# Mamba-style scan block: the first sums of a chunk in two pieces, TensorE's side work in other slots, x loaded before the end of the scan phase

## The chip, the core and the metric

The kernel runs on one core of a Trainium2 chip. The metric is the time of one execution on the device, in microseconds (us), median of several runs. The core has five engines that run their own instruction streams and meet at semaphores: TensorE (PE; its weight loads are shown as PEld), VectorE (DVE), ScalarE (ACT), GpSimd (POOL) and SyncE (SP, which here only issues DMAs).

## What is computed

Eight images of 64x64 tokens with 96 channels go through two layers. The first is a selective state-space scan over four orders of the tokens (diagonal, anti-diagonal, and both backwards), the second a linear attention and a quantised feed-forward part. Only the scan matters for this change:

```python
def step(hst, inp):
    u_t, d_t, B_t, C_t = inp
    hst = hst * jnp.exp(d_t[..., None] * A) + (d_t * u_t)[..., None] * B_t[:, :, None, :]
    return (hst, jnp.einsum('bkdn,bkn->bkd', hst, C_t))
```

with 192 channels d, 16 states n, 4 orders k and 4096 tokens t. The decay is exp(d_t A), the drive is (d_t u_t) B_t, and the output is a sum over the 16 states of state times C_t.

## The kernel before, in words

**Tiling.** For each image the scan phase runs over 4 orders times 8 chunks of 512 tokens: 32 chunks an image, 256 in all. In a chunk the 192 x 16 pairs of channel and state are dealt with in 12 steps (`NSTEP`), each of two scans on 128 partitions (4 states x 32 channels). `GROUPS` says which 32 channels a step has: 4, 5, 0, 1, 2, 3 and again 4, 5, 0, 1, 2, 3. Groups 4 and 5 are the high channels, and their sums go to PSUM bank 5; groups 0 to 3 are the low ones, and go to bank 4. A group takes the 32 rows 32g (or 32(g-4)) of its bank, and so the 32 columns of TensorE's array with that number.

**One step.** ACT makes the decays (L671, two exponentials a step, three steps ahead of use); PE makes the drive (`fill`, L1002, 32 small matmuls, shown as 64 records since each float32 matmul has two), DVE runs the two scans (L1370), POOL multiplies the states by C (L484). PE then sums products over the states (`sum_states`, L1026): a batch is four steps, and each of its two halves a = 0, 1 is one call of four matmuls. After the sixth call of a chunk DVE adds the result to the image's output (`add_sums`, L1349 to L1357; it stands in DVE's stream between the two scans of step 5 of the next chunk, and waits for the semaphore `summed`).

**Order on PE.** PE's stream of a chunk has 12 slots. Slot s begins with the fill of step s + 2 (the fills of steps 0 and 1 of the next chunk in slots 10 and 11), since two steps fit into PSUM at once: that fill waits until DVE has scanned step s. Behind it stands the side work that the code hands to the slot: for the next chunk the projections (`project_lo` L959, `project_hi` L964, one for the high channels, v = 0, and one for the low, v = 1), the turned B (`turn_b`, L975), the turned product du (`turn_du`, L984); and the sums, by the table `SUM_SLOTS`, slot to (batch, a), where slots from `NSTEP` on are those of the next chunk. So before the change the slots hold, beside a fill each: 0 project_hi 0; 1 sum (2,0) of the chunk before; 2 turn_b; 3 project_hi 1 and sum (2,1) of the chunk before; 4 nothing; 5 sum (0,0); 6 turn_du 0; 7 sum (0,1); 8 turn_du 1; 9 project_lo 0; 10 sum (1,0); 11 sum (1,1) and project_lo 1.

**ACT beside the decays.** In slot 4 of its own stream it saves the turned B (L631), runs the two softplus (L615, each after its project_hi; between exponential and softplus it loads a table), and issues the DMAs that replicate the high channels' delta (L648). SP writes B to memory in a skewed layout (L375) when ACT has saved it, reads it back (L382), replicates the other delta (L399) and C (L390).

**Ends of the phase.** Before the first chunk of an image, `pre` runs the same side work with nothing to hide it. After the last chunk all engines meet (`rendezvous`), SP loads the image's x into `xtok` (L354), which lies on the same memory as `delta_rep`, and PE's first transposes of it (L1074) open the next phase.

Of the kernel before, what the change touches and what calls it, by code (L numbers as in the profile page):

```python
# [29 lines left out]
NCH = L // T  # L30
# [29 lines left out]
def build(nc, io, out, nb=B):  # L60
    ctx = ExitStack()
    with ctx:
# [99 lines left out]
        def rendezvous(eng, b, ph):  # L162

            eng.drain().then_inc(phase_done, 1)  # L164
            wait_apart(eng, phase_done, b * (NPH * ENGINES) + (ph + 2) * ENGINES)
# [100 lines left out]
            return bank(SMALL)[0:rows, at:at + cols]  # L266

        Y_BANK, HI_BANK, LO_BANK = 4, 6, 7
        SUM_SLOTS = {5: (0, 0), 7: (0, 1), 10: (1, 0), 11: (1, 1), NSTEP + 1: (2, 0), NSTEP + 3: (2, 1)}

        GROUPS = (4, 5, 0, 1, 2, 3) * NPR
        BT_ROWS = slice(DHI, P)
# [42 lines left out]
        def chunks(eng, b, body, pre):  # L315


            def at(kk, c, par, first=False):
                ch = Chunk(b, kk, c, first)
                ch.par = par  # L320
                return ch
            order = [at(kk, c, c % 2, kk == 0 and c == 0) for kk in range(K) for c in range(NCH)] + [None, None]
            pre(order[0], order[1])
            for ch, nx, then in zip(order, order[1:], order[2:]):
                body(ch, nx, then, 0 if ch.c == 0 else 1 if ch.c + 1 < NCH else 2)
# [3 lines left out]
        def _(sp):  # L329
# [27 lines left out]
            def load_x(sp, b):  # L357
                for c in range(NCH):
                    load_part(b, c)

            def image(b, f):
# [44 lines left out]
                    load_c(1)  # L406

                chunks(sp, b, lambda ch, nx, then, kind: prepare(nx) if nx else None, lambda ch, nx: prepare(ch))
                rendezvous(sp, b, 1)

                load_x(sp, b)
                wait_apart(sp, x_loaded, (b * 2 + 2) * (16 * NCH))
                if f is not None:
                    for c in range(NCH):
# [145 lines left out]
        def _(act):  # L560
# [44 lines left out]
            def image(b, f):  # L605
# [43 lines left out]

                def pre(ch, nx):  # L650
                    copy_bc(ch)
                    softplus(ch, 0)
                    softplus(ch, 1)
                    load_delta(ch, 4)
                    load_delta(ch, 5)
                    save_bt(ch)
                    save_du(ch, 0)
                    save_du(ch, 1)
                    for s in range(AHEAD):
                        decays(ch, s)  # L660
# [237 lines left out]
        def _(pe):  # L898
# [53 lines left out]
            def image(b, f):  # L952
# [8 lines left out]
                def project_hi(ch, v):  # L961

                    z = 1 - v
                    pe.matmul(bank(HI_BANK + v), xw_hi[:, ch.k, z * P:(z + 1) * P], u_hi[:, bass.ds(ch.t0, T)], start=False, stop=True).then_inc(pre_filled, 1)  # L964
# [50 lines left out]
                    project_lo(nx, 0)  # L1015
                    project_lo(nx, 1)

                def sum_states(ch, batch, a):

                    if batch == 0 and a == 0 and not ch.first:  # L1020
                        pe.wait_ge(y_saved, ch.n(2, 0))
                    pe.wait_ge(weighted, ch.n(NSTEP, 4 * batch + 4))
                    for s in range(4 * batch, 4 * batch + 4):
                        g = GROUPS[s]
                        bk, row = (Y_BANK, CW * g) if g < 4 else (Y_BANK + 1, CW * (g - 4))
                        mm = pe.matmul(bank(bk)[row:row + CW, :], gather[:, :], ch.weighed(s, a),  # L1026
                                       start=(s < NG and a == 0), stop=(s >= NG and a == 1))
                    if a == 1:
                        mm.then_inc(summed, 1)

                def body(ch, nx, then, kind):
                    if not ch.first:
                        kk, c = (ch.kk, ch.c - 1) if kind else (ch.kk - 1, NCH - 1)
                        before = Chunk(ch.b, kk, c)
                        before.par = 1 - ch.par
                    for s in range(NSTEP):
                        if s + 2 < NSTEP:
                            fill(ch, s + 2)
                        elif nx:
                            fill(nx, s + 2 - NSTEP)  # L1040
                        if nx:
                            if s == 0:
                                project_hi(nx, 0)
                            if s == 3:
                                project_hi(nx, 1)
                            if s == 2:
                                turn_b(nx)
                            if s == 6:
                                turn_du(nx, 0)
                            if s == 8:  # L1050
                                turn_du(nx, 1)
                            if s == 9 and then:
                                project_lo(then, 0)
                        if s in SUM_SLOTS:
                            sum_states(ch, *SUM_SLOTS[s])
                        if not ch.first and s + NSTEP in SUM_SLOTS:
                            sum_states(before, *SUM_SLOTS[s + NSTEP])
                        if s == NSTEP - 1 and then:
                            project_lo(then, 1)
                    if nx is None:  # L1060
                        sum_states(ch, 2, 0)
                        sum_states(ch, 2, 1)
# [558 lines left out]
```

## Time and profile before

| | before |
|---|---|
| median of 3 runs | 11323.54 us (11293.52 to 11373.81) |
| the profiled execution | 11306.72 us, its span 11304.9 us |
| TensorE clock granted, mean | 0.927 |
| PE busy | 9638.9 us, 85% |
| DVE busy | 8620.7 us, 76% |
| POOL busy | 7841.6 us, 69% |
| ACT busy | 6486.2 us, 57% |
| chain that ended last, by engine | PE 55%, issue 14%, DVE 11%, POOL 9% |

A row of the groups names line, engine, operation, what it writes and reads, its count, the time in which any of the group ran, the mean of one, then the idle time of the engine ahead of the group and what ended it. "issue" is idle time that no semaphore explains. The TensorE clock has two levels here, 2.4 GHz (1.0) and 1.2 GHz (0.5).

### The profile page before, as it was taken

How to read it: one execution, taken by the hardware profiler on the slowest of the kernel's cores; microseconds unless marked ns; L12 is line 12 of the kernel's file. 1: busy time of each engine (PE TensorE's matmuls, PEld its weight loads, DVE VectorE, ACT ScalarE, POOL GpSimd, SP SyncE). 2: the span in 40 equal slices, each digit the busy share in tenths (PEclk: the TensorE clock that was granted, in tenths of full speed). 3: DMA queues.
4: the chain of work that ended last, by engine and by line, in shares of the span. 5: the costliest groups of instructions: out<-in, count | busy, mean ns of one | idle time of the engine just before them, and what ended most of it. 6: DMA issues, size and time to landing. Idle time of an engine off the chain costs nothing.

```text
span 11304.9 us, 500467 instructions
## 1 busy us (share of the span) xinstructions
PE 9638.9 (85%) x224288; PEld 4968.1 (44%) x224288; DVE 8620.7 (76%) x8404; ACT 6486.2 (57%) x9893; POOL 7841.6 (69%) x4027
## 2 busy tenths in 40 slices
PE   7888888888888888888888888898888888888886
PEld 3444344443444434444344443444434444344443
DVE  4898668986589856899568895698956888478884
ACT  4666556665566645666456664566645666456664
POOL 3888538885488854888458884588845888458883
PEclk9999899998999989999889998899989999899997
DMA  3555225552255523555135551355513555145550
GB/s 90 148 147 147 64 77 143 149 141 62 81 142 153 141 55 84 147 149 152 40 96 144 147 148 38 98 146 148 147 35 110 146 143 145 28 116 149 143 144 22
DMA packets 853330, 1301.52 MB, mean 115 GB/s; under 512 B 517231, under 2 KB 518800, under 8 KB 785148
## 3 DMA queue, kind: packets, MB, share of 16 engines
q1 hardware_dynamic: 752892, 1135.15, 36.1%
q10 hardware_dynamic: 98304, 134.35, 4.5%
q8 instruction: 1776, 29.10, 1.2%
q14 instruction: 358, 2.93, 0.1%
HBM read 832.67 MB, written 33.55 MB: 77 GB/s over the span
## 4 chain that ended last, share of the span: by engine, by line
PE 55%; issue 14%; DVE 11%; POOL 9%; SPq 4%; ACT 3%; DMA 2%; ACTq 2%; POOLq 1%; DVEq 0%
PE ps L1002 22%; PE ps L1026 13%; DVE arena L1370 8%; PE ps L934 5%; PE ps L964 5%; POOL arena L484 5%; PE ps L959 4%; SPq L399 3%; PE ps L975 2%; ACTq L648 2%; ACT arena L671 1%; PE ps L984 1%; POOL arena L501 1%; POOL arena L509 1%; POOL arena L536 1%
## 5 line engine op out<-in xcount | busy, mean ns | idle before, releaser
L1370 DVE TENSOR_TENSOR_SCAN arena<-arena,ps 128x512 f32<-128x512 f32 x6144 | 7259.5, 1251 | 899.9 <-PE ps L1002 887.2
L484 POOL TENSOR_TENSOR arena<-arena 128x1024 f32<-128x1024 f32 x3072 | 6613.4, 2185 | 1414.1 <-DMA arena<-c_rows 979.4
L671 ACT ACTIVATE arena<-arena,negA 128x512 f32<-128x512 f32 x6144 | 3952.1, 714 | 1755.5 <-DMA arena<-arena 831.6
L1002 PE MATMUL ps<-arena 64*32 64x128 f32 x196608 | 3966.2, 284 | 1046.9 <-issue 479.5
L1002 PEld LDWEIGHTS ps<-arena 64*32 64x32 f32 x196608 | 2965.3, 107 | 3024.5 <-issue 2997.1
L1026 PE MATMUL ps<-arena,gather 128*32 128x512 f32 x12288 | 2207.4, 631 | 66.9 <-POOL arena L484 50.4
L934 PE MATMUL ps<-arena,wconv 96*64 96x512 f32 (+1 forms) x2304 | 835.9, 629 | 23.7 <-issue 23.7
L469 POOL TENSOR_TENSOR arena<-arena,u_hi 128x512 f32<-128x512 f32 x256 | 327.8, 1280 | 696.1 <-ACT arena L615 696.1
L1026 PEld LDWEIGHTS ps<-arena,gather 128*32 128x32 f32 x12288 | 374.4, 111 | 992.5 <-issue 808.8
L964 PE MATMUL ps<-u_hi,xw_hi 128*128 128x512 f32 x1024 | 671.0, 742 | 3.0 <-issue 3.0
L671 ACT ACT_TABLE_LOAD x256 | 328.4, 1283 | 557.9 <-issue 557.7
L959 PE MATMUL ps<-u_lo,xw_lo 128*128 128x512 f32 x1024 | 589.6, 660 | 55.2 <-SPq L164 47.2
L615 ACT ACTIVATE arena<-ps,dtb 128x512 f32<-128x512 f32 x512 | 341.8, 688 | 341.8 <-PE ps L964 338.2
L934 PEld LDWEIGHTS ps<-arena,wconv 96*64 96x64 f32 (+1 forms) x2304 | 301.9, 172 | 415.4 <-issue 407.9
L469 POOL TENSOR_TENSOR arena<-arena,u_lo 128x512 f32<-128x512 f32 x256 | 328.9, 1285 | 115.8 <-PE ps L984 101.9
L515 POOL TENSOR_TENSOR arena<-arena,power 128x4 f32<-128x4 f32 x64 | 64.8, 1013 | 425.7 <-DVE arena L1401 425.7
L639 ACT ACTIVATE arena<-ps 128x256 f32<-128x256 f32 (+1 forms) x512 | 247.0, 484 | 175.0 <-PE ps L984 174.4
L975 PE MATMUL ps<-ident,arena 16*64 16x16 f32 x4096 | 297.1, 209 | 48.3 <-issue 39.1
L615 ACT ACT_TABLE_LOAD x256 | 328.4, 1283 | 4.7
L984 PE MATMUL ps<-ident,arena 64*128 64x64 f32 (+1 forms) x2048 | 290.4, 264 | 41.5 <-POOL arena L469 34.0
L531 POOL TENSOR_TENSOR arena<-arena 128x1056 f32<-128x1056 f32 x16 | 64.4, 4024 | 372.0 <-DVE arena L1430 372.0
L975 PEld LDWEIGHTS ps<-ident,arena 16*64 16x64 f32 x4096 | 270.7, 138 | 115.2 <-issue 115.2
(155 smaller groups left out, 5648.4 us busy)
## 6 DMA issues: line engine op xcount, KB each, us to landing
arena<-b_runs SPq DMA_DIRECT2D x512, 1024.0 KB, 7.0
arena<-arena SPq DMA_DIRECT2D x4096, 64.0 KB
arena<-c_rows SPq DMA_DIRECT2D x2048, 128.0 KB, 3.8
arena<-arena ACTq DMA_DIRECT2D x2048, 64.0 KB
arena<-in_x SPq DMA_DIRECT2D x128, 192.0 KB, 2.7
out_tokens<-arena SPq DMA_DIRECT2D x64, 192.0 KB, 2.4
c_rows<-arena SPq DMA_DIRECT2D x256, 32.0 KB
b_runs<-arena SPq DMA_DIRECT2D x512, 16.0 KB
```

The costliest lines, as they stand in the source:

```text
L469: pool.tensor_tensor(du.rearrange("p (k h t) -> p h k t", h=2, k=NB), in_time(t_l[v]), in_time(u_lo[:, ch.dir, cols] if v else u_hi[:, col ...
L484: pool.tensor_tensor(ch.weighed(s)[:, :, flip], ch.span(s)[:, :, flip], c_row[:, :, flip], ALU.mult).then_inc(weighted, 1)
L615: act.activation(t_l[v], bank(HI_BANK + v), ACT.Softplus, bias=dtb[:, 1 - v, ch.k:ch.k + 1]).then_inc(delta_done, 1)
L671: act.activation(ch.span(s, a), delta_rep[:, g, :], ACT.Exp, scale=negA[:, ch.k, i:i + 1]).then_inc(decay_ready, 1)
L934: return pe.matmul(to.rearrange("p (r w) -> p r w", w=W), wconv[:, t, channels], xT_img[:, r0:r0 + ROWS, dx:dx + W], start=(t == 0), stop= ...
L959: pe.matmul(bank(HI_BANK + v), xw_lo[:, ch.k, z * P:(z + 1) * P], u_lo[:, ch.dir, bass.ds(ch.t0, T)], start=True, stop=False)
L964: pe.matmul(bank(HI_BANK + v), xw_hi[:, ch.k, z * P:(z + 1) * P], u_hi[:, bass.ds(ch.t0, T)], start=False, stop=True).then_inc(pre_filled, 1)
L975: mm = pe.matmul(to, bc_raw[r, steps(h, k)], ident[r, ch.d0:ch.d0 + NS].rearrange("p (q n) -> p q n", n=RUN), start=True, stop=True)
L984: mm = pe.transpose(bank(HI_BANK + v)[:, k * w:(k + 1) * w], du[r, k * P:(k + 1) * P], ident[r, r])
L1002: mm = pe.matmul(to, du_t[ch.par][rows, k, g * CW:(g + 1) * CW], spots[rows, j, :, :], start=True, stop=True)
L1026: mm = pe.matmul(bank(bk)[row:row + CW, :], gather[:, :], ch.weighed(s, a), start=(s < NG and a == 0), stop=(s >= NG and a == 1))
L1370: dve.tensor_tensor_scan(ch.span(s, a)[:, flip], ch.span(s, a)[:, flip], drive(s % 2)[:, :, a][:, flip], before, ALU.mult, ALU.add).then_i ...
```

## The change

Four edits:

1. `SUM_SLOTS`: the sums of the first batch (steps 0 to 3) go in pieces. Piece `half` 0 is steps 0 and 1 (groups 4, 5: high channels), piece 2 is steps 2 and 3 (groups 0, 1). (0,0) has its pieces in slots 5 and 6, (0,1) in slots 7 and 8. The semaphore `summed` is raised behind piece 2. The last sum (2,1) of the chunk before moves from slot 3 to slot 2.
2. PE's other side work: turn_b from slot 2 to 3, project_hi 1 from 3 to 4, turn_du 1 from 8 to 9.
3. `pre` on ACT: the turned B is saved right behind the copy of B and C, and the first half of du ahead of the delta DMAs.
4. SP: x is loaded when the last decays of the image have been made (they are the last to read `delta_rep`), ahead of the rendezvous.

```diff
-        SUM_SLOTS = {5: (0, 0), 7: (0, 1), 10: (1, 0), 11: (1, 1), NSTEP + 1: (2, 0), NSTEP + 3: (2, 1)}
+        SUM_SLOTS = {5: (0, 0, 0), 6: (0, 0, 2), 7: (0, 1, 0), 8: (0, 1, 2), 10: (1, 0), 11: (1, 1), NSTEP + 1: (2, 0), NSTEP + 2: (2, 1)}
...
+                wait_apart(sp, decay_ready, (b + 1) * (K * NCH * NCOL))
+                load_x(sp, b)
                 rendezvous(sp, b, 1)
 
-                load_x(sp, b)
...
                     copy_bc(ch)
+                    save_bt(ch)
                     softplus(ch, 0)
                     softplus(ch, 1)
+                    save_du(ch, 0)
                     load_delta(ch, 4)
                     load_delta(ch, 5)
-                    save_bt(ch)
-                    save_du(ch, 0)
                     save_du(ch, 1)
...
-                def sum_states(ch, batch, a):
-
-                    if batch == 0 and a == 0 and not ch.first:
+                def sum_states(ch, batch, a, half=None):
+
+                    if batch == 0 and a == 0 and half == 0 and not ch.first:
                         pe.wait_ge(y_saved, ch.n(2, 0))
                     pe.wait_ge(weighted, ch.n(NSTEP, 4 * batch + 4))
-                    for s in range(4 * batch, 4 * batch + 4):
+                    for s in range(4 * batch + (half or 0), 4 * batch + (4 if half is None else half + 2)):
...
-                    if a == 1:
+                    if a == 1 and half != 0:
                         mm.then_inc(summed, 1)
...
                             if s == 3:
+                                turn_b(nx)
+                            if s == 4:
                                 project_hi(nx, 1)
-                            if s == 2:
-                                turn_b(nx)
                             if s == 6:
                                 turn_du(nx, 0)
-                            if s == 8:
+                            if s == 9:
                                 turn_du(nx, 1)
```

On PE, in a chunk of the running loop, from slot 2 to the fill of slot 8, there stood before (L1002 fill, L975 turn_b, L964 project_hi, L1026 sum, L984 turn_du; x64 are two fills):

```order
L1002 MATMUL ps<-arena 32x128 x32
L975 MATMUL ps<-ident,arena 64x2x8 x8
L1002 MATMUL ps<-arena 32x128 x32
L964 MATMUL ps<-u_hi,xw_hi 128x512
L1026 MATMUL ps<-arena,gather 32x512 x4
L1002 MATMUL ps<-arena 32x128 x64
L1026 MATMUL ps<-arena,gather 32x512 x4
L1002 MATMUL ps<-arena 32x128 x32
L984 MATMUL ps<-ident,arena 128x64 x4
L1002 MATMUL ps<-arena 32x128 x32
L1026 MATMUL ps<-arena,gather 32x512 x4
L1002 MATMUL ps<-arena 32x128 x32
```

Now there stands, from slot 2 to the fill of slot 7 (all lines are one higher behind the added line):

```order
L1003 MATMUL ps<-arena 32x128 x32
L1027 MATMUL ps<-arena,gather 32x512 x4
L1003 MATMUL ps<-arena 32x128 x32
L976 MATMUL ps<-ident,arena 64x2x8 x8
L1003 MATMUL ps<-arena 32x128 x32
L965 MATMUL ps<-u_hi,xw_hi 128x512
L1003 MATMUL ps<-arena 32x128 x32
L1027 MATMUL ps<-arena,gather 32x512 x2
L1003 MATMUL ps<-arena 32x128 x32
L985 MATMUL ps<-ident,arena 128x64 x4
L1027 MATMUL ps<-arena,gather 32x512 x2
L1003 MATMUL ps<-arena 32x128 x32
```

The last sum of the chunk before stands one fill, a turn_b and a project_hi earlier; the slot that had a fill alone has a project_hi; two calls of four matmuls are four calls of two.

On ACT, ahead of an image's first chunk (L624 copy of B and C, L615 softplus, L648 the delta DMAs, L631 save of the turned B, L639 saves of du, L671 decays), before:

```order
L624 ACTIVATE arena<-ps 32x512
L615 ACT_TABLE_LOAD
L615 ACTIVATE arena<-ps,dtb 128x512 x2
L648 DMA arena<-arena 32x512 x8
L631 ACTIVATE arena<-ps 64x128
L639 ACTIVATE arena<-ps 128x4x64
L639 ACTIVATE arena<-ps 128x4x128
```

and now:

```order
L625 ACTIVATE arena<-ps 32x512
L632 ACTIVATE arena<-ps 64x128
L616 ACT_TABLE_LOAD
L616 ACTIVATE arena<-ps,dtb 128x512 x2
L640 ACTIVATE arena<-ps 128x4x64
L649 DMA arena<-arena 32x512 x8
L640 ACTIVATE arena<-ps 128x4x128
```

The save of the turned B stands ahead of a table load, two softplus and eight DMA issues behind which it stood.

On SP, at the end of the scan phase (L354 loads of x), with the semaphores that each waits for, before (-) and now (+):

```order
 L390 DMA arena<-c_rows 32x1024 x3
-L354 DMA arena<-in_x 128x4x96 [waits phase_done]
+L354 DMA arena<-in_x 128x4x96 [waits decay_ready]
 L354 DMA arena<-in_x 128x4x96 x7
-L354 DMA arena<-in_x 128x4x96 [waits x_loaded,d_x1]
+L354 DMA arena<-in_x 128x4x96 [waits phase_done,x_loaded,d_x1]
```

The eight loads of x passed the rendezvous; nothing else of SP's stream moved past them.

## Rows read from the trace of the kernel before

**Rows 1.** Windows: PE, PEld, DVE, ACT, POOL busy, PEclk, DMA share, GB/s.

```profile
183.66:1256.15 1072.49, 941.78 (x27024) 510.90 (x27008) 949.11 (x830) 660.77 (x1012) 896.89 (x444) 0.96 0.52 144
215.23:250.19 34.96, 30.36 (x856) 15.79 (x848) 29.76 (x28) 22.28 (x35) 31.69 (x17) 0.95 0.52 141
349.69:380.41 30.72, 28.25 (x852) 15.54 (x848) 29.81 (x27) 20.87 (x33) 29.17 (x16) 1.00 0.57 160
```

**Rows 2.** Groups by line, whole span: the loop's four largest on PE, DVE, POOL.

```profile
L1370 DVE TENSOR_TENSOR_SCAN arena<-arena,ps 128x512 f32<-128x512 f32 x6144 | 7259.5, 1251 | 899.9 <-PE ps L1002 887.2 <-issue 1.0 <-ACT arena L671 0.2
L484 POOL TENSOR_TENSOR arena<-arena 128x1024 f32<-128x1024 f32 x3072 | 6613.4, 2185 | 1414.1 <-DMA arena<-c_rows 979.4 <-DVE arena L1370 432.0
L1002 PE MATMUL ps<-arena 64*32 64x128 f32 x196608 | 3966.2, 284 | 1046.9 <-issue 479.5 <-DVE arena L1370 410.9 <-DMA arena<-b_runs 122.9
L1026 PE MATMUL ps<-arena,gather 128*32 128x512 f32 x12288 | 2207.4, 631 | 66.9 <-POOL arena L484 50.4 <-issue 15.6
```

**Rows 3.** Groups by line: the first instruction of DVE's add_sums, whole span.

```profile
L1349 DVE SCALAR_TENSOR_TENSOR y_d<-u_lo,dsum,ps 128x512 f32<-128x512 f32 x64 | 47.8, 748 | 87.8 <-PE ps L1026 87.8
L1356 DVE TENSOR_TENSOR y_d<-ps,y_d 128x512 f32<-128x512 f32 x64 | 44.3, 692 | 70.9 <-PE ps L1026 70.9
L1352 DVE COPY u_lo<-ps 128x512 f32<-128x512 f32 x64 | 44.3, 692 | 80.9 <-PE ps L1026 80.9
L1356 DVE TENSOR_TENSOR u_lo<-ps,u_lo 128x512 f32<-128x512 f32 x64 | 44.2, 690 | 116.5 <-PE ps L1026 116.5
```

**Rows 4.** Critical chain of a chunk at full clock: start us, us, what.

```profile
731.00 1.18 PE ps L1002 x63
732.18 1.84 PE ps L1026 x8
734.02 1.12 PE ps L1002 x62
...
751.91 1.00 PE ps L1026 x8
...
757.32 1.04 PE ps L1026 x8
...
759.82 1.29 DVE arena L1370
```

**Rows 5.** Timeline, same image, a fill that stops half way: start, us, engine, line.

```profile
229.56 0.65 PE L1002 MATMUL ps<-arena 64*32 64x128 f32 x9 [2.55 <-issue]
230.15 2.07 PE L964 MATMUL ps<-u_hi,xw_hi 128*128 128x512 f32 x2
```

**Rows 6.** Timeline just behind it: second softplus, scans from (5,1), decays of step 8.

```profile
232.26 0.69 ACT L615 ACTIVATE arena<-ps,dtb 128x512 f32<-128x512 f32 x1 [3.98 <-PE ps L964]
...
234.94 9.46 DVE L1370 TENSOR_TENSOR_SCAN arena<-arena,ps 128x512 f32<-128x512 f32 x8
...
236.74 0.73 ACT L671 ACTIVATE arena<-arena,negA 128x512 f32<-128x512 f32 x1
```

**Rows 7.** Timeline ahead of the second image's first scan.

```profile
1558.53 1.07 PE L975 MATMUL ps<-ident,arena 16*64 16x16 f32 x16 [0.77 <-ACT arena L624]
...
1561.63 5.02 ACTq L648 DMA_DIRECT2D arena<-arena  x8
...
1566.70 0.27 ACT L631 ACTIVATE arena<-ps 64x128 f32<-64x128 f32 x1 [4.46 <-issue]
...
1569.19 2.56 ACT L671 ACTIVATE arena<-arena,negA 128x512 f32<-128x512 f32 x4
...
1579.68 1.22 DVE L1370 TENSOR_TENSOR_SCAN arena<-arena,ps 128x512 f32<-128x512 f32 x1 [25.61 <-PE ps L1002]
```

**Rows 8.** Timeline behind the second image's last scan.

```profile
2668.65 4.60 SPq L354 DMA_DIRECT2D arena<-in_x  x8
...
2676.48 1.91 PE L1074 MATMUL ps<-ident,arena 128*96 128x128 f32 x8 [9.46 <-DMA arena<-in_x]
2677.58 0.78 ACT L718 ACTIVATE arena<-ps,gsm 96x512 f32<-96x512 f32 x1 [30.50 <-PE ps L1074]
```

## The prediction

> **What bounds the kernel now.** I read the windows first. The scan phase of the first image takes 1072.49 us, and there are eight of them, some 8580 of 11305 us; that is 33.5 us a chunk. Two chunks stand beside it: one at full clock takes 30.72 us, one with the clock at 0.95 takes 34.96 us, and PE is busy some 28 to 30 us in both, DVE just under 30, POOL 29 to 32 [rows 1]. The reader is to see that no engine has 2 us to spare in a short chunk, and that a long one is long with DVE doing no more in it.
>
> Then the groups: the scans wait 899.9 us, nearly all for fills, and fills wait 410.9 us for scans and 479.5 us for nothing that the profile names [rows 2]. Each engine waits for the other, so there is a loop between them. The chain of waits shows it. PE alone carries it from 731.00 to 758.36, where the last sum of the chunk before ends; then DVE adds, scans (5,1) until 761.11, and the next fill of PE follows some 0.14 us later [rows 4]. In that round only the fill of slot 4 lies beside DVE's part. So PE works 27.4 us on the chain and 1.1 beside it, 28.5 in all, and the round takes 30.25: PE stands still for 1.8 us a chunk since the last sum comes late. The group row says the same, 410.9 / 256 = 1.6 us. DVE waits there as well: the four kinds of first addition wait 87.8 + 70.9 + 80.9 + 116.5 = 356 us for that sum [rows 3], 1.4 us a chunk.
>
> The rest of a chunk is of two kinds. Fills stop half way for "issue": 479.5 / 256 = 1.9 us a chunk, as the 2.55 us in [rows 5]. Behind such a stop the clock is at its lower level: the projection there takes 2.07 us. The granted clock of 0.96 over the phase is 8% of it at the lower of two levels, 2.7 us a chunk, in which half the work is lost: 1.35 us. The account is 28.5 + 1.8 + 1.9 + 1.35 = 33.5, against the 33.5 measured. So PE bounds the loop, with 1.8 us of standing still that the order causes.
>
> **The last sum one slot earlier.** It now stands ahead of fill 5, turn_b and project_hi 1, and ends some 3.2 us sooner in PE's stream (a fill 1.12 [rows 4], two operations of about 1 us). The additions waited 1.4 us for it, so they are found ready: the wait of [rows 3] goes to nothing, and with it the detour over DVE. What is late next: PE alone (28.5 us) or DVE alone. DVE needs 24 scans at 9.46 / 8 = 1.18 us [rows 6], 28.4, and about 1.4 for the additions, 29.8 us. In a chunk without a stop DVE is then the bound, and the gain is only 30.25 - 29.8 = 0.4 us, or a little more where small waits sit. In a chunk with a stop PE is the bound, and up to 1.8 us come free. Chunks of 30.7 and of 35 us average 33.5 only if more than half have a stop, so I take the mean near 1.2 us before the costs below.
>
> **The pieces.** A sum of batches 1 and 2 has four different column groups and takes 1.00 us, one of batch 0 has groups 4, 5, 0, 1, that is two column groups twice, and takes 1.84 us [rows 4]. With r for a round of matmuls that run side by side and o for what a block costs besides, 2r + o = 1.00 and 4r + o = 1.84: r = 0.42, o = 0.16. A piece is two rounds, 1.0 us. Four pieces instead of two calls cost 2 x 0.16 = 0.3 us more of PE a chunk. The page "TensorEngine Tiling" of the Trainium skill (Key Properties) says that changing the tiling mode drains TensorE; the trace agrees that a block has a fixed cost, and puts it at 0.16 us. The pieces even out the slots: fill and side work took 1.12 + 1.84 = 3.0 us in slots 5 and 7 against 2.4 us of a step's scans, and now 2.1 in slots 5, 7 and 8, 2.5 in slot 6. The heavy ones are now 9 (about 2.8) and, as before, 11. The product of step 3, for which the first piece still waits, was hardly ever late: 50.4 us over the whole run [rows 2].
>
> **Softplus and what follows.** project_hi 1 comes a sum and a fill later, 2.1 us. ACT waits for it in its stream: behind it are the second softplus, a table load, and the decays of step 8. In the chunk of [rows 6] these decays start at 236.74 and the first is there at 237.5, while scan (8,0), the sixth of the eight, starts at 234.94 + 5 x 1.18 = 240.8: 3.4 us to spare. Take 2.1 off, and 1.5 to 2 since DVE has come forward, and they are 0.2 to 0.7 us late; in a chunk without a stop the reserve is some 2 us larger. I put 0.3 us on half the chunks, at most 0.2 on the mean. The turned B is saved a slot later, which moves its write and read; the fill that needs it comes eight slots on, and I take nothing, with the b_runs waits of now, 122.9 us [rows 2], as the bound to be doubled. turn_du 1 a slot later is used two slots on: nothing. `summed` of batch 0 is raised at about the same time, since its slot 7 started late behind a long slot 5.
>
> Loop: 1.2 - 0.2 for what the pieces and ACT cost beyond what DVE-bound chunks hide = about 0.9 to 1.0; I take **0.9 us x 256 = 230 us**. Bounds: 0, if what is freed is lost elsewhere, and 1.8 us, 460 us, if the detour goes everywhere.
>
> **Before the first scan.** The turned B is there at 1559.6 and saved at 1566.70, 7.1 us later, behind softplus and DMA issues of 5.02 us [rows 7]. It carries the chain: write, read back, first fill, scan after 25.61 us of idle DVE. Now it is saved at once. Next in line are the decays: 1569.19, and now some 1.5 us later, as the table load is no longer hidden and a save stands ahead of the DMAs; the first is done near 1571.5, and the scan, 7.1 us earlier, starts at 1572.6. So the decays are ready just before it, and I take **7.1 us x 8 = 57 us**; bounds 4 us each, if the decays slip behind the delta DMAs, and 8, where the two meet.
>
> **x.** Eight loads are issued at 2668.65 and the first transpose starts at 2676.48; ACT made its last decay 30.5 us before 2677.58, at 2647 [rows 8]. The loads now start there, 21 us ahead of the rendezvous, and are hidden by the last scans and sums. SP has nothing else queued then. The transposes start at once, and all of the phase moves: **7.7 us x 8 = 61 us**. It costs nothing as long as 8 us of loads fit into 21.
>
> **Sum.** 230 + 57 + 61 = 348 us off the profiled 11306.7 gives 10959. That execution lies 17 us under the median of the runs, so on their scale it is 10975 us, 3.1% less. The rivals' times are on that scale too.
>
> **Rivals.**
> *The falls of the clock go too.* Each long chunk costs 4 us more than a short one [rows 1], half of it by the clock. The page "TensorE: Matmul & The Clock Gate" of the Trainium skill (Part 1) says that idle time brings the lower clock; by rows, the fall in [rows 5] comes behind PE's own stop, and PE stood still a second time, 1.8 us, a few us on. If the second standing tips the balance in half of the falls, their 1.35 us becomes 0.7, and with the detour gone wholly the loop gains 1.8 + 0.7 - 0.3 = 2.2, less 0.3 for DVE-bound chunks, 1.9 us: 486 + 118 = 604 us off, 10720. Against it: most falls follow stops of 2 to 3 us that stay. Chance 0.18.
>
> *The gain is eaten.* POOL is busy 29 to 32 us a chunk [rows 1] and its products wait 979.4 us for C [rows 2]; if a period of 32.5 us is one that POOL and the queue of SP can't follow, the loop gives nothing and only 118 us remain: 11206. Against it: the chunk of 30.72 us shows them following. Chance 0.16.
>
> *A block costs more than 0.16.* If a change of tiling leaves nothing side by side, a block costs a whole matmul, 631 ns [rows 2]: two more blocks take 2 x (0.63 - 0.16) = 0.9 us a chunk, and again 11206. For it speaks only that a block of two rounds was never seen beside column pairs. Chance 0.07.
>
> *Slower: the decays of step 8 become the wait.* If the 0.2 to 0.7 us of above are 2.4, a slot, in every chunk, DVE loses 614 us of the scans: 10975 + 614 = 11590. It turns the sign from 1.4 us a chunk on. Against it: ACT is busy 21 to 22 of 31 to 35 us [rows 1], and scans waited 0.2 us for decays in all [rows 2]. Chance 0.05.
>
> The forecast has 0.50; 0.04 are for others.
>
> **Numbers.** Low end: the case of the clock, 10700. High end: just under the cases that leave 118 us, 11190. Differences under 1%, about 113 us, are what a measurement of this kernel can hardly tell from none. 11206 is near that bound; I give half of those cases to each side: faster 0.50 + 0.18 + 0.12 + 0.02 = 0.82, within 1% 0.12, slower 0.06.
>
> **What would show it.** In the changed kernel the wait ahead of the first addition falls from 356 us to under 50, and the fills' waits for scans fall from 410.9 to about 250 or less. "issue" ahead of fills stays near 480, and the clock in the phase near 0.96; if it rises to 0.98, it is the first rival. Scans that wait for L672 for more than 50 us speak for the last one. Sums on PE take some 80 us more in all; 240 would be the third. Save of the turned B follows turn_b at once, DVE is idle some 18 us ahead of the first scan instead of 25.6, and L1074's wait for x is gone. The prediction is wrong if chunks without a stop still take 30.7 us and chunks with one still 35.

## The result, and the profile after

The changed kernel is slower by 0.6%. Its median is 11362.2 us (11327.7 to 11401.15, 13 runs) against 11295.3 us for the kernel before on the same chips (13 runs): ratio 1.0059, 95% interval 1.0037 to 1.0081. The forecast was 3.1% faster.

The two ends of the phase did what they were meant to, and the loop more than lost it. From the last scan of an image to the first of the next, the mean over seven stretches fell from 327.7 to 311.8 us, the tail behind the last scan from 243.2 to 230.3, the head by 5.6: about 130 us less in all. The loop, first scan to last scan of an image, mean of eight, rose from 1073.0 to 1095.4 us: 179 us more in all. That is 34.2 us a chunk for 33.5. The two add up to the 49 us by which the span grew.

The page and the groups by line of the changed kernel (columns as before; every line number behind the added line is one higher):

```profile
span 11353.9 us, 500475 instructions
PE 9720.2 (86%) x224288; PEld 5013.3 (44%) x224288; DVE 8636.1 (76%) x8404; ACT 6462.0 (57%) x9893; POOL 7813.8 (69%) x4027
PE 24%; SPq 20%; issue 13%; POOL 13%; DMA 11%; ACTq 8%; ACT 5%; DVE 5%; POOLq 1%; DVEq 0%
```

The third line is the chain that ended last. PE carried 55% of it before and carries 24% now; SP's queue, the landing of DMAs and ACT's queue have 39%. The same work is done by the same instructions, so the time has gone into who waits for whom:

```profile
L1371 DVE TENSOR_TENSOR_SCAN arena<-arena,ps 128x512 f32<-128x512 f32 x6144 | 7309.1, 1254 | 1317.8 <-PE ps L1003 856.3 <-ACT arena L672 449.2
L1003 PE MATMUL ps<-arena 64*32 64x128 f32 x196608 | 4054.0, 293 | 962.3 <-DMA arena<-b_runs 477.7 <-issue 242.2 <-DVE arena L1371 235.5
L616 ACT ACTIVATE arena<-ps,dtb 128x512 f32<-128x512 f32 x512 | 350.4, 688 | 856.6 <-PE ps L965 853.2
L1350 DVE SCALAR_TENSOR_TENSOR y_d<-u_lo,dsum,ps 128x512 f32<-128x512 f32 x64 | 46.2, 722 | 0.0
L1357 DVE TENSOR_TENSOR u_lo<-ps,u_lo 128x512 f32<-128x512 f32 x64 | 42.8, 669 | 70.8 <-PE ps L1027 70.8
```

Against [rows 3], the additions no longer wait: 71 us in all for 356. Against [rows 2], the fills' waits for scans fell from 411 to 236 us and those for "issue" from 480 to 242. But fills now wait 478 us for the read of B (123 before), the softplus waits 853 us for its projection (338 before), and the scans wait 449 us for decays (0.2 before): 167 us of that is ahead of the first scans, and 269 us is at step 8.

The granted clock of the loop is 0.925 for 0.958. In the inner 30 chunks of the images (without the first and the last of each) it fell 234 times for 131, and 215 of the 234 times while DVE was in step 5.

### The profile page after: what moved, and what is told of

It reads as the page before. It is cut to its first block, busy times and chain, and to the rows that moved or that the text cites. A ratio compares the mean times of both kernels' runs of the same rounds, so it can differ in the third digit from the quotient of the medians.

```text
span 11353.9 us, 500475 instructions
## 1 busy us (share of the span) xinstructions
PE 9720.2 (86%) x224288; PEld 5013.3 (44%) x224288; DVE 8636.1 (76%) x8404; ACT 6462.0 (57%) x9893; POOL 7813.8 (69%) x4027
## 3 DMA queue, kind: packets, MB, share of 16 engines
q8 instruction: 1776, 29.10, 1.1%
## 4 chain that ended last, share of the span: by engine, by line
PE 24%; SPq 20%; issue 13%; POOL 13%; DMA 11%; ACTq 8%; ACT 5%; DVE 5%; POOLq 1%; DVEq 0%
SPq L399 17%; DMA arena<-b_runs 9%; POOL arena L485 8%; ACTq L649 8%; PE ps L1003 8%; PE ps L935 5%; PE ps L965 4%; SPq L390 3%; ACT arena L672 3%; PE ps L1027 3%; DVE arena L1371 3%; DMA arena<-c_rows 1%; POOL arena L502 1%; POOL arena L510 1%; PE ps L960 1%
## 5 line engine op out<-in xcount | busy, mean ns | idle before, releaser
L1003 PE MATMUL ps<-arena 64*32 64x128 f32 x196608 | 4054.0, 293 | 962.3 <-DMA arena<-b_runs 477.7
L1003 PEld LDWEIGHTS ps<-arena 64*32 64x32 f32 x196608 | 3066.9, 110 | 3513.7 <-issue 3502.9
L965 PE MATMUL ps<-u_hi,xw_hi 128*128 128x512 f32 x1024 | 779.7, 853 | 0.0
L960 PE MATMUL ps<-u_lo,xw_lo 128*128 128x512 f32 x1024 | 562.8, 633 | 54.5 <-SPq L164 47.1
L1027 PEld LDWEIGHTS ps<-arena,gather 128*32 128x32 f32 x12288 | 318.8, 109 | 549.3 <-issue 382.2
```

What stands on the lines that cost most here:

```text
L960: pe.matmul(bank(HI_BANK + v), xw_lo[:, ch.k, z * P:(z + 1) * P], u_lo[:, ch.dir, bass.ds(ch.t0, T)], start=True, stop=False)
L1003: mm = pe.matmul(to, du_t[ch.par][rows, k, g * CW:(g + 1) * CW], spots[rows, j, :, :], start=True, stop=True)
```

## The experiments

Each kernel ran beside the kernel before on the same chip; ratios are to it, with 95% intervals. "Loop" is first to last scan of an image, mean of eight, from the profiled execution. Falls of the clock are those in the inner 30 chunks of the images.

| kernel | ratio | loop, us | fills <- b_runs, issue, us | falls of the clock |
|---|---|---|---|---|
| before | 1 | 1073.0 | 123, 480 | 131 |
| changed | 1.0059 (1.0037 to 1.0081) | 1095.4 | 478, 242 | 234 |
| e_ends | 0.9902 (0.9871 to 0.9933) | 1074.7 | 37, 465 | 146 |
| e_sum_early | 0.978 (0.9727 to 0.9833) | 1060.4 | 57, 450 | 115 |
| e_hi_late | 1.0107 (1.0068 to 1.0145) | 1091.4 | 468, 306 | 184 |
| e_b1_first | 1.0008 (0.9986 to 1.003) | 1093.8 | 25, 596 | 145 |
| e_hi_slot3 | 0.9807 (0.9765 to 0.985) | 1063.2 | 155, 464 | 151 |
| e_back | 0.9737 (0.9699 to 0.9775) | 1056.3 | 57, 424 | 112 |
| e_whole | 1.0071 (1.0046 to 1.0097) | 1100.8 | 537, 243 | 229 |
| e_small_c | 0.9545 (0.9503 to 0.9588) | 1015.5 | 98, 274 | 50 |
| e_ring_c0 | 0.9898 (0.9856 to 0.994) | 1079.6 | 32, 714 | 163 |
| e_back_c0 | 0.9833 (0.9797 to 0.9869) | 1069.2 | 19, 462 | 127 |
| e_ring_act | 0.9722 (0.9695 to 0.9749) | 1055.6 | 30, 585 | 134 |
| e_pre2 | 0.9726 (0.9702 to 0.9749) | 1059.5 | 55, 423 | 110 |

### First set: which edit costs the loop

**e_ends.** The kernel before with

```diff
+                wait_apart(sp, decay_ready, (b + 1) * (K * NCH * NCOL))
+                load_x(sp, b)
                 rendezvous(sp, b, 1)
-                load_x(sp, b)
...
                     copy_bc(ch)
+                    save_bt(ch)
...
+                    save_du(ch, 0)
                     load_delta(ch, 4)
```

> The kernel before with edits 3 and 4 alone (the saves of `pre` and the early x); the loop is that of before. In the trace of the changed kernel an image's stretch between its last scan and the next image's first scan fell from a mean of 328 to 312 us, and the tail from 243 to 230. If these two edits give that by themselves, this kernel takes 11295 - 130 = 11165 us, ratio 0.9885, with the loop at 1072 us an image. Rival: part of the 130 us is lost again in the loop, since the first chunk's DMAs now meet others; then the ratio is 0.993 or more and the loops are longer than 1072.

0.9902, and the loop is the old one (1074.7). The ends give 111 us by the ratio. They didn't cost the loop anything.

**e_sum_early.** e_ends with

```diff
-        SUM_SLOTS = {5: (0, 0), 7: (0, 1), 10: (1, 0), 11: (1, 1), NSTEP + 1: (2, 0), NSTEP + 3: (2, 1)}
+        SUM_SLOTS = {5: (0, 0), 7: (0, 1), 10: (1, 0), 11: (1, 1), NSTEP + 1: (2, 0), NSTEP + 2: (2, 1)}
```

> The kernel before with edits 3 and 4, and of the loop only the last sum (2,1) one slot earlier; turn_b, project_hi 1 and turn_du 1 stay, and the first sums stay whole. Theory A (the queue): the late project_hi 1 is what cost the loop, by way of ACT and of SP's queue, and the early sum in itself is good: the wait ahead of the first addition goes to under 60 us, fills' waits for b_runs stay near 120, the loop gains 0.5 to 0.9 us a chunk, ratio 0.97 to 0.977. Theory B (PE's stops set the period, the early sum only moves the wait): the loop stays at 1072 us, ratio that of e_ends, 0.9885.

0.978: as theory A said, just short of its range. The early sum is good in itself. Its gain in the loop, 14.3 us an image or 0.45 us a chunk, is half of what was forecast. Against e_ends, the wait ahead of the additions fell from 411 to 51 us, but the scans' wait for fills rose from 638 to 887, so two thirds of the wait came back at the next fill. And PE's own wait for scans fell by little, to 389 us from 447:

```profile
L1003 PE MATMUL ps<-arena 64*32 64x128 f32 x196608 | 3967.8, 284 | 979.0 <-issue 464.7 <-DVE arena L1371 446.5 <-DMA arena<-b_runs 36.9
L1003 PE MATMUL ps<-arena 64*32 64x128 f32 x196608 | 3956.6, 284 | 924.3 <-issue 449.9 <-DVE arena L1371 389.3 <-DMA arena<-b_runs 57.4
```

The first row is of e_ends, the second of e_sum_early.

**e_hi_late.** The kernel before with one line moved:

```diff
-                            if s == 3:
+                            if s == 4:
                                 project_hi(nx, 1)
```

> The kernel before with one line moved: project_hi 1 of the next chunk from slot 3 to slot 4; nothing else. Theory A (the queue): decays of steps 8 to 11 come later, SP's delta and C transfers with them, the second half of B lands after the fill of step 6 wants it: waits of fills for b_runs rise from 123 to over 300 us, the granted clock falls to 0.91, and the time rises by 100 us or more, ratio 1.01 to 1.03, though the last sum itself ends 1 us sooner as nothing stands ahead of it. Theory C (pieces) and D (the turned B in its later slot): these are not in here, so the ratio is 0.97 to 1.0 with the gain of the sooner sum.

1.0107, with the waits and the chain (PE 24%, SP's queue 22%) of the changed kernel, and nearly its loop:

```profile
L1002 PE MATMUL ps<-arena 64*32 64x128 f32 x196608 | 4004.6, 288 | 990.9 <-DMA arena<-b_runs 468.3 <-issue 306.4 <-DVE arena L1370 197.0
```

One projection behind a fill instead of ahead of it makes this kernel 1.1% slower. Neither the pieces nor the turned B are in here. The clock of the loop is 0.947, not the 0.91 expected.

**e_b1_first.** The changed kernel with

```diff
                     load_delta(0)
+                    load_b(1)
                     load_delta(1)
                     load_c(0)
-                    load_b(1)
```

> The changed kernel, with SP issuing the load of B's second half ahead of delta's second part and of C, for which it would have to wait for the last decays. Theory A (the queue): the fill of step 6 no longer waits for b_runs (478 us before, now under 100), PE is not idle there, the clock recovers above 0.92, and the time falls by 150 to 400 us under the changed kernel: ratio to the kernel before 0.97 to 0.99. Theory C (pieces) or D (turned B): the fill waits for something else and the ratio stays at 1.00 to 1.01.

A miss: the waits for b_runs did vanish (25 us), but the time is 1.0008, only 0.5% under the changed kernel.

```profile
L1003 PE MATMUL ps<-arena 64*32 64x128 f32 x196608 | 3991.2, 285 | 917.4 <-issue 595.7 <-DVE arena L1371 287.2 <-DMA arena<-b_runs 25.3
L485 POOL TENSOR_TENSOR arena<-arena 128x1024 f32<-128x1024 f32 x3072 | 6609.8, 2187 | 1582.5 <-DMA arena<-c_rows 1327.5 <-DVE arena L1371 253.2
```

The fills stop for "issue" instead, 596 us for 242, and the products still wait 1328 us for C (1424 in the changed kernel), which stands in SP's queue behind the same delta transfers. The move also gave SP a wait that the changed kernel doesn't have. B's second half may be loaded over only when the last fill of the running chunk has read it, so SP now waits for that fill with half of the delta transfers and C behind:

```profile
SPq L160 <- PE ps L1003: 267.0, 123, 6.4
```

So the wait for B alone could be a symptom, and that had to be tried from other sides.

### The round

The timeline of the changed kernel shows what the moved projection has closed: a round, that is, a path of waits that leads from an operation back to the same operation one chunk later. Start, us, engine, line; the second softplus of a chunk to that of the next:

```profile
735.05 0.69 ACT L616 ACTIVATE arena<-ps,dtb 128x512 f32<-128x512 f32 x1 [1.92 <-PE ps L965]
735.21 2.50 ACTq L649 DMA_DIRECT2D arena<-arena  x4
737.74 1.28 ACT L672 ACT_TABLE_LOAD   x1 [2.00 <-issue]
...
739.03 0.73 ACT L672 ACTIVATE arena<-arena,negA 128x512 f32<-128x512 f32 x1
...
741.93 3.79 ACT L672 ACTIVATE arena<-arena,negA 128x512 f32<-128x512 f32 x6 [1.56 <-issue]
...
743.45 12.87 SPq L399 DMA_DIRECT2D arena<-arena  x16
...
756.50 1.84 SPq L390 DMA_DIRECT2D arena<-c_rows  x4
758.53 0.34 SPq L382 DMA_DIRECT2D arena<-b_runs  x1
...
767.00 1.97 PE L1003 MATMUL ps<-arena 64*32 64x128 f32 x64 [2.92 <-DMA arena<-b_runs]
...
768.90 2.08 PE L965 MATMUL ps<-u_hi,xw_hi 128*128 128x512 f32 x2
...
771.01 0.69 ACT L616 ACTIVATE arena<-ps,dtb 128x512 f32<-128x512 f32 x1 [4.62 <-PE ps L965]
```

Behind the second softplus ACT issues DMAs, loads its table, and makes the decays of steps 8 and 9. SP waits for those of step 9, then issues 16 delta transfers, which take 12.9 us of its queue, then C, then at 758.53 the load of B's second half. That lands 8 us later, the fill of step 6 starts at 767.00, and project_hi 1 stands behind it on PE. ACT's softplus of the next chunk stands behind that. The three softplus in this stretch start at 703.18, 735.05 and 771.01, 33.9 us apart on the mean; the loop takes 34.2 a chunk. Before, project_hi 1 stood ahead of this fill, and a late B could delay the fill but not the softplus.

Two counts over all chunks but the first and the last ones of each image bear this out. First, the parts of the round, means of 232 chunks: from the start of the second softplus to the end of step 9's decays 7.7 us, from there to the load of B's second half 15.0, its landing 6.9, from there to the fill of step 6 0.7, fill and projection 4.0. The sum is the period of 34.3 us by construction; what tells is that only the 0.7 us of it is slack, and that the fill waits for B in 172 of 256 chunks. In the kernel before, it starts 4.8 us after B has landed, and waits in 24. Second, the chunks with a stop for "issue" of more than 0.5 us ahead of a fill and those without one: before, they take 34.1 and 31.7 us on the mean (188 and 52 chunks), in the changed kernel 34.3 and 34.3 (118 and 122), in e_hi_late 34.2 and 34.1. PE's own stops no longer set how long a chunk takes, so what sets it lies outside them.

While PE stands still the clock goes as well:

```profile
763.00:766.90 3.90, 1.09 (x20) 0.99 (x16) 3.84 (x5) 2.54 (x4) 3.90 (x3) 0.86 0.65 151
767.00:770.90 3.90, 3.90 (x66) 2.01 (x66) 2.08 (x3) 0.00 (x0) 3.90 (x3) 0.50 0.36 76
```

PE is busy 1.09 us of the first 3.9 us, and the next 3.9 us have the lower of the two clock levels, 0.50. The fill takes 1.97 us and the projection 2.08.

### Second set: opening or shortening the round on each of its engines

**e_hi_slot3, on PE.** The changed kernel with

```diff
                             if s == 3:
                                 turn_b(nx)
-                            if s == 4:
                                 project_hi(nx, 1)
```

> The changed kernel, with project_hi 1 back in slot 3, behind turn_b, so that on PE it stands ahead of the fill of step 6 instead of behind it; all else as changed. The traces of the changed kernel and of e_hi_late show a closed round: fill of step 6, project_hi 1, second softplus, decays of step 9, twelve us of SP's delta issues, the load of B's second half, fill of step 6 of the next chunk. Theory A' (that round sets the loop's time): putting the projection ahead of the fill opens it; fills' waits for b_runs fall from 478 to under 150 us, the loop from 1095 to 1055 to 1070 us an image, the ratio to the kernel before is 0.97 to 0.985. Rival (it is the later turned B, or the pieces, that hold the loop): 1.000 to 1.006 as the changed kernel.

0.9807: 2.5% off the changed kernel for one operation that changes places with one fill. The fills' waits for b_runs fall to 155 us, the softplus waits 2 us, and chunks with and without a stop differ again (33.6 and 32.2 us).

**e_ring_act, on ACT.** The changed kernel with

```diff
                         if nx and s == 4:
                             save_bt(nx)
+                        if nx and s == 6:
                             softplus(nx, 0)
                             softplus(nx, 1)
                             load_delta(nx, 4)
-                        if nx and s == 5:
+                        if nx and s == 7:
                             load_delta(nx, 5)
```

> The changed kernel, with ACT running both softplus and the delta DMAs of the high channels two slots later in its own stream, behind the decays of steps 8 and 9 instead of ahead of them; the save of the turned B stays in slot 4. PE and SP are as changed. In the changed kernel ACT stands still for project_hi 1 (853 us) with these decays queued behind it; here it makes them while it waits, and SP's delta issues follow the softplus more closely. If the round over ACT and SP's queue sets the loop, it loses the decays (1.4 us each step) and part of the table load: waits of scans for decays of step 8 (269 us) vanish, waits for b_runs fall from 478 to under 250 us, loop 1050 to 1075 us an image, ratio 0.97 to 0.99. If the loop is held elsewhere, ratio 1.000 to 1.006; if softplus now comes too late for POOL's product with u and the turned du, above 1.006.

0.9722, at the good end of the range. PE's stream is that of the changed kernel to the last instruction, project_hi 1 behind the fill included. With the decays of steps 8 and 9 ahead of the softplus and no longer behind it, they are made while ACT would stand still. SP's waits for decays, and for the softplus:

```profile
SPq L160 <- ACT arena L672: 377.6, 243, 15.5
SPq L160 <- ACT arena L616: 340.0, 245, 3.2
```

The first is 2210.0 us in the changed kernel and 1648.3 in the kernel before; the second is 0.8 us in the changed kernel. So the round isn't open here, since SP still waits for the softplus and that for the projection. It is shorter: the delta issues start 0.8 us after the start of the second softplus, for 7.9, and the fill of step 6 starts 4.2 us after B has landed, for 0.7.

**e_ring_c0, on SP.** The changed kernel with

```diff
+                    load_c(0)
                     load_delta(0)
                     load_delta(1)
-                    load_c(0)
                     load_b(1)
```

> The changed kernel, with SP issuing the first half of C (four DMAs, 2 to 2.6 us of its queue) ahead of both delta parts, where what it waits for is long done; all waits stay, only the order of SP's stream changes. If the round fill 6, project_hi 1, softplus, decays, SP's queue, B's second half sets the loop's 34.2 us a chunk, it is shorter by these 2 us until the next bound: loop 1040 to 1065 us an image, b_runs waits from 478 to under 250, ratio 0.965 to 0.985. If the waits for b_runs are only a symptom and something else sets the loop (as e_b1_first, where they vanished and the time stayed, could be read), ratio 1.000 to 1.006.

0.9898, 1.6% off the changed kernel but less than expected: loop 1079.6. Waits for b_runs fell to 32 us, and the fill of step 6 starts 3.9 us after B has landed, so the round no longer sets the period. What does is not settled. Stops for "issue" rose to 714, and scans still wait 167 us for the decays of step 8 (269 in the changed kernel). And what C waits for is not "long done", as was expected: its place may be written only when POOL has made the product of step 5, and SP now waits for that with all delta transfers behind:

```profile
SPq L160 <- POOL arena L485: 486.2, 287, 4.7
```

In the changed kernel it is 9.6 us.

**e_whole.** The changed kernel with

```diff
-        SUM_SLOTS = {5: (0, 0, 0), 6: (0, 0, 2), 7: (0, 1, 0), 8: (0, 1, 2), 10: (1, 0), 11: (1, 1), NSTEP + 1: (2, 0), NSTEP + 2: (2, 1)}
+        SUM_SLOTS = {5: (0, 0), 7: (0, 1), 10: (1, 0), 11: (1, 1), NSTEP + 1: (2, 0), NSTEP + 2: (2, 1)}
```

> The changed kernel with the first sums whole again, in slots 5 and 7; the moves of the last sum, turn_b, project_hi 1 and turn_du 1, and the two ends, stay. If the round over SP's queue sets the loop, the pieces don't matter here: the ratio stays at 1.000 to 1.008, b_runs waits near 478 us. If the pieces cost the loop (rival), it falls to 0.98 to 0.99.

1.0071: with the round closed the pieces don't matter. The moves of turn_b, project_hi 1 and turn_du 1 are all in here, the pieces are not.

Together: e_hi_late and e_hi_slot3 show by the time that the place of this one projection is the cause, e_ring_act that it costs by way of ACT and what follows, and the two counts above that the period is the round's. One thing isn't separated. The late decays of step 8 also hold the scans without SP in between, and e_hi_slot3 and e_ring_act remove that wait (269 us) together with the one for B. In e_b1_first, where B is early and the projection late, it is 51 us, so most of it seems to follow from the late B.

**e_back.** The changed kernel with turn_b and project_hi 1 back where they were:

```diff
+                            if s == 2:
                                 turn_b(nx)
-                            if s == 4:
+                            if s == 3:
                                 project_hi(nx, 1)
```

> The changed kernel with turn_b and project_hi 1 both back in slots 2 and 3: against e_sum_early it has the four pieces and turn_du 1 in slot 9. Pieces at 0.3 us a chunk of PE's time, as worked out, would make it 80 us slower than e_sum_early where PE is the bound, ratio 0.985; if a piece's even spread is worth more than its block cost, 0.965 to 0.975; at 0.6 us a block, 0.99 to 0.995.

0.9737, 3.2% under the changed kernel. Against e_sum_early (0.978) the intervals overlap: the pieces and the later turn_du cost nothing that can be told. On PE a block of a piece lasts 1.05 us, a whole call of batch 0 1.91, one of the other batches 1.07 (medians): 0.2 us more a call, 0.4 a chunk, about the 0.3 worked out. Against e_hi_slot3 (0.9807) the later turned B seems to cost something as well, 7 us an image in the loops. The intervals of the ratios overlap, but both kernels ran on the same chip, and all four runs of e_back (11009 to 11030 us) lie under all four of e_hi_slot3 (11072 to 11116).

### What stops the fills half way

**e_small_c.** The kernel before with

```diff
+                            if ch.first:
                                 sp.dma_start(c_rep[pr][j * CW:(j + 1) * CW, :], rows[j:j + 1, :].to_broadcast([CW, 2 * T])).then_inc(c_loaded[pr], 16)
+                            else:
+                                sp.dma_start(c_rep[pr][j * CW:j * CW + 1, :], rows[j:j + 1, :]).then_inc(c_loaded[pr], 16)
```

> The kernel before, with C replicated only for the first chunk of each image; in the other 31 its eight DMAs are issued at the same places, each to one partition instead of 32, so that 1 MB less moves in a chunk. Left out: C of those chunks, their output is not the reference's. It asks what stops the fills half way (issue, 480 us): if it is the traffic of the DMA queues, through which PE's code comes as well, issue falls under 250 us, falls of the clock from 131 to under 70, ratio 0.96 to 0.98. If the stops have another cause, issue stays at 400 to 500 and the ratio at 0.99 to 1.0 (products no longer wait for C, 979 us).

```profile
PE ps L1005 <- issue: 273.5, 312, 4.3
```

0.9545, more than expected, with the stops a little above the 250 named. With 1 MB less a chunk the stops fall from 480 to 274 us, the falls of the clock from 131 to 50. So a part of the stops seems to come from the traffic on the DMA queues. The sum of the stops alone doesn't prove it, since it is as low, 242 us, in the changed kernel with all its traffic, where PE waits for B instead; but here no other wait of the fills grew to match: for scans it is 482 us (411 before). That PE's code is what is late there is an inference: the page lists instructions as a DMA kind of their own (1776 packets), but no row ties a stop to one of them.

**e_back_c0.** e_back with C's first half ahead of both delta parts, as in e_ring_c0.

> e_back (0.974) with the same move of C's first half in SP's stream. POOL's products waited 862 us for C there; if POOL's start in a chunk still holds the loop through the sums and the decays that wait for them, the loop falls from 1056 to 1035 to 1050, ratio 0.960 to 0.970. If PE's own stops set it, the ratio stays at 0.971 to 0.977; if C now meets B's first half on the DMA queues and the code of PE starves more, issue rises above 450 us and the ratio is above 0.977.

0.9833: worse than e_back by 1%. The products no longer wait for C (862 us to nothing), which gained nothing, so POOL's wait was free. Scans wait 947 us for fills instead of 846, stops for "issue" rise only from 424 to 462. What grew most is the wait of the move itself, as in e_ring_c0:

```profile
SPq L160 <- POOL arena L485: 1161.8, 306, 5.9
```

SP stands 1162 us for POOL's product of step 5 with the delta transfers behind it, and the decays' wait for landed data rises from 586 to 702 us. That this is the 1% is likely, not shown.

**e_pre2.** e_back with `save_du(ch, 0)` in `pre` behind `load_delta(ch, 5)` again.

> e_back (ratio 0.974) with one more change ahead of the first chunk: the first half of du is saved behind the delta DMAs again, the turned B stays first. In the changed kernel the first scan waits for the first decay, which waits for these DMAs, issued 2.3 us later than before; with them earlier the idle time of DVE there falls from 20.9 to 18 to 19.5 us, 12 to 20 us over eight images, 0.1 to 0.2%: ratio 0.970 to 0.975, not to be told from e_back by its time, only by the row of that wait.

0.9726, not to be told from e_back, as expected. The first scans wait 153 us for decays in all, 19.1 an image, where e_back has 167, 20.9 an image; so it does what was meant.

## Why the prediction was wrong

**What held.** The last sum's early end removed the wait ahead of the additions: 71 us of 356 remain, about the 50 forecast. A block costs about what was worked out, and both ends of the phase gain.

**The step that failed is "Softplus and what follows".** It followed the late project_hi 1 to the decays of step 8 and to the scan that reads them, found them 0.2 to 0.7 us late on some chunks, and stopped at 0.2 us a chunk. Two things were left out. First, who else waits for those decays: SP, whose stream is in order, waits for the decays of step 9 with 16 delta transfers, C and B's second half behind. Second, what that does to PE: project_hi 1 now stands behind the very fill that needs this B. The prediction said the projection comes "a sum and a fill later, 2.1 us", and never asked what the fill waits for. Measured, the move costs 1.1% alone (e_hi_late). Where its projection is put back ahead of the fill, the changed kernel gains 2.5% (e_hi_slot3), some 285 us, where 0.2 us x 256 = 51 us were set.

**The row that was read as a reserve.** "scans waited 0.2 us for decays in all" and "the b_runs waits of now, 122.9 us [rows 2], as the bound to be doubled" are waits of one order of the streams. They say how much was late, not how far the rest is from being late. The b_runs waits became four times as long. The slower rival had the right place, the decays of step 8, but its price was worked out as a delay of DVE alone, and it got 0.05. Its sign did come: scans wait 282 us for decays beside the 167 ahead of the first scans, where over 50 were to speak for it.

**The main term was too large by half.** Without the closed round the loop gains 0.45 us a chunk by the early sum (e_ends to e_sum_early) and 0.57 to e_back, with the pieces in, where 0.9 was forecast. Here the failed term is the detour: the prediction's sum put PE's wait for scans, 410.9 / 256 = 1.6 us a chunk, down to the late last sum, and let "up to 1.8 us come free" in a chunk with a stop. With the sum early and nothing else of the loop changed, that wait only fell from 447 to 389 us (250 or less was forecast), and chunks with a stop of over 0.5 us got 0.65 us shorter (34.0 to 33.3), those without one not at all (32.2 and 32.5, some 50 chunks each, too few to tell them apart). The scans took back 249 of the 360 us by waiting for the next fills. The total of e_back, 2.6%, is near the 3.1% forecast partly by luck: by the profiles, its loops gave 134 us for 230 and the ends 143 for 118.

**Before the first scan** 5.4 us an image came instead of 7.1. The read of B was indeed earlier, but the first decays took over:

```profile
1563.45 0.27 ACT L632 ACTIVATE arena<-ps 64x128 f32<-64x128 f32 x1 [1.25 <-PE ps L976]
...
1567.76 5.29 ACTq L649 DMA_DIRECT2D arena<-arena  x8
...
1573.46 3.67 PE L1003 MATMUL ps<-arena 64*32 64x128 f32 x128 [3.18 <-DMA arena<-b_runs]
...
1577.81 2.56 ACT L672 ACTIVATE arena<-arena,negA 128x512 f32<-128x512 f32 x4 [2.82 <-DMA arena<-arena]
1578.64 2.33 DVE L1371 TENSOR_TENSOR_SCAN arena<-arena,ps 128x512 f32<-128x512 f32 x2 [20.83 <-ACT arena L672]
```

Against [rows 7], the turned B is saved at once, but the fill stands ready at 1577.1 and the scan waits for a decay, which waits for delta: its DMAs start 6.1 us behind the start of the copy of B and C, 3.8 before, and meet the read of B. I had the decays follow their issue, not their landing.

**x** went as said at its place: the transposes start with the phase. From the last scan of an image to the first transpose it takes 15.8 us on the mean before and 8.2 in e_ends, 7.6 less for the 7.7 forecast; in the changed kernel it is 10.6.

```profile
2678.09 4.02 POOL L502 COPY arena<-y_hi 128x512 f32<-128x512 f32 x4 [5.48 <-DVEq L164]
2678.12 1.91 PE L1075 MATMUL ps<-ident,arena 128*96 128x128 f32 x8 [1.82 <-DVEq L164]
```

The wait of 7.7 us of [rows 8] is gone.

**Of the rivals**, the clock went the other way (0.925): 215 of its 234 falls come in step 5, where PE stands still for B. With the round open it did go a little the rival's way, 0.967 in the loops of e_back for 0.958. The eaten gain was right that SP's queue can't follow, though not about POOL; the dearer block is refuted.

## What to carry to other kernels

When an operation is moved behind another in an engine's stream, write down what the one it is now behind waits for, and follow both ends round: who waits for the moved one, down every in-order queue, until the path ends or comes back. A path that comes back is a round whose length is the period, and no reserve read from the old trace speaks of it. If it does come back, it can be opened or made shorter than the period on any engine on it: here a projection ahead of a fill, or two decays ahead of a softplus, gave 2.5% and 3.4%, and the latter with PE's order left as it was. A sign of such a round is that chunks with and without a stop take the same time. Before a transfer is moved forward in an in-order queue, write down what it waits for itself, since all behind it will wait as well: two such moves gained 0.5% and 1.6%, and one lost 1%.

A removed wait is worth what the next wait leaves of it: here a third.

## What the chip did that was not expected

Moving 1 MB less a chunk, with the same number of DMA issues, took 4.5% off (e_small_c), nearly half of PE's stops that no semaphore explains (480 to 274 us) and more than half of the falls of the clock (131 to 50). These stops shrink where PE waits for something else (242 us in the changed kernel) and come back when that wait goes, with or without a transfer moved: 464 us in e_hi_slot3, 585 in e_ring_act, 596 in e_b1_first, 714 in e_ring_c0. Why the last three lie above the 480 of the kernel before is open. Sixteen issues of 64 KB take 12 to 13 us of SP's queue, which is more than the load of 1 MB that stands behind them needs to land (6.9 us).
